# Score differences from subtracted keys, later transposes, a spread split, and top-k values multiplied once a batch

## The reference, cut to what matters

```
x = x + attn_a(ln(x))     # 16 heads of 8: softmax(q k^T) v over 1024 tokens, then Wo
x = x + ffn(ln(x))        # 128 -> 512 -> 512 -> 128, signs as weights, relu between
x = x + attn_b(ln(x))     # 8 heads of 16, windows of 64 tokens, top 32 of each by distance
x = x + ffn(ln(x))
# attn_b, per batch, head and token t
q, v   = relu(x @ encoder_query), relu(x @ encoder_value)
metric = softplus(base + 0.1 * mlp(mean of q))
dist   = sqrt(sum((q[window] - q[t])**2 * metric) + 1e-8)
top 32 nearest: w = exp(-dist) / sum;  context = sum(w * v[of those tokens])
context += gate * 0.1 * (q / |q|) @ (U V);  out = q * context;  out @ decoder
```

## Time and profile before

| | us |
|---|---|
| median of 3 executions (3197.55 to 3203.15) | 3201.6 |
| profiled execution, its own time | 3204.65 |
| its span, first to last instruction | 3202.8 |
| first batch's maximum phase, up to the exponentials | 102.7 |
| a middle batch: maximum phase | 189.0 |
| a middle batch: exponential phase | 174.9 |
| tail behind the last exponential | 294.7 |

### The profile page before, as it was taken

One profiled execution on the slowest core, in us unless ns is written; L12 is line 12 of the kernel. 1 busy time (PEld: TensorE's weight loads), 2 busy tenths in 40 slices (PEclk: granted clock), 3 DMA queues, 4 the chain that ended last, 5 costly groups with the idle time before them and its releaser, 6 DMA issues.

```text
span 3202.8 us, 73054 instructions
## 1 busy us (share of the span) xinstructions
PE 2629.4 (82%) x22579; PEld 1200.3 (37%) x22579; DVE 2128.0 (66%) x10282; ACT 2331.6 (73%) x3225; POOL 618.0 (19%) x797
## 2 busy tenths in 40 slices
PE   5878778889788888888879888898978888887666
PEld 2212243344333443334433344333433344333444
DVE  5701668846776668856689466885677666892595
ACT  4697569967698667976689666996669866795433
POOL 2010013101131112401132011311123111221232
PEclk6599689999899998999989998999989998999888
DMA  2011001000010000100000000000001000000000
GB/s 80 14 36 31 2 1 38 28 15 6 9 35 29 11 6 9 48 22 8 2 33 29 17 9 9 32 28 16 5 9 39 29 10 2 9 2 1 1 8 8
DMA packets 60585, 58.20 MB, mean 18 GB/s; under 512 B 15218, under 2 KB 41524, under 8 KB 60196
## 3 DMA queue, kind: packets, MB, share of 16 engines
q1 hardware_dynamic: 59952, 52.95, 5.3%
q10 hardware_dynamic: 244, 0.39, 0.0%
HBM read 35.66 MB, written 17.56 MB: 17 GB/s over the span
## 4 chain that ended last, share of the span: by engine, by line
PE 40%; ACT 24%; issue 20%; DVE 10%; POOL 4%; SPq 2%; ACTq 0%; DMA 0%; DVEq 0%; POOLq 0%
PE banks L756 37%; ACT PT L1097 11%; ACT pq L1084 3%; POOL Aop L735 2%; DVE pq L1217 2%; PE banks L763 1%; ACT h L1109 1%; ACT xn L1046 1%; DVE xn L1434 1%; DVE h L1437 1%; ACT hparts L1108 1%; ACT h L1156 1%; POOL qkf L709 1%; PE banks L988 1%; SPq L520 1%
## 5 line engine op out<-in xcount | busy, mean ns | idle before, releaser
L1097 ACT ACTIVATE PT<-banks 128x1024 f32<-128x1024 f32 x1024 | 996.4, 1035 | 47.9 <-PE banks L756 38.9
L1217 DVE CUSTOM_DVE_ANT_0 pq<-pq,banks 128x512 f32<-128x512 f32 x1024 | 660.2, 685 | 269.6 <-ACT pq L1084 241.7
L1084 ACT ACTIVATE pq<-banks 128x1024 f32<-128x1024 f32 x512 | 523.5, 1022 | 337.3 <-PE banks L756 328.4
L756 PE MATMUL banks<-K,Q 48*128 48x512 bf16 x3072 | 494.8, 435 | 87.3 <-ACT pq L1084 65.2
L756 PE MATMUL banks<-PT,Vg 128*32 128x512 f32 x4096 | 560.2, 620 | 2.0 <-ACT PT L1097 2.0
L756 PE MATMUL banks<-Q,K 51*128 51x512 bf16 x2048 | 397.6, 396 | 168.0 <-ACT PT L1097 158.8
L719 POOL TENSOR_TENSOR hparts<-h,hparts 128x512 fp32r<-128x512 f32 x112 | 140.3, 1272 | 1152.1 <-ACT h L1109 1152.0
L1434 DVE MATCH_REPLACE8 xn<-h,xn 128x96 f32<-128x96 f32 x1536 | 352.6, 243 | 0.0
L756 PEld LDWEIGHTS banks<-Q,K 51*128 51x128 bf16 x2048 | 108.8, 93 | 590.4 <-issue 560.3
L756 PE MATMUL banks<-hparts,W 128*128 128x512 f32 x1024 | 301.9, 423 | 27.6 <-ACT h L1109 21.7
L756 PEld LDWEIGHTS banks<-K,Q 48*128 48x128 bf16 x3072 | 127.6, 100 | 399.4 <-issue 341.4
(11 more groups left out here) (200 smaller groups left out, 3412.7 us busy)
## 6 DMA issues: line engine op xcount, KB each, us to landing
scratch_qk<-pq SPq DMA_DIRECT2D x24, 512.0 KB, 2.7
qkf<-in_hidden_states SPq DMA_DIRECT2D x16, 512.0 KB, 3.9
Q<-scratch_qk SPq DMA_DIRECT2D x126, 48.0 KB
K<-scratch_qk SPq DMA_DIRECT2D x126, 48.0 KB
Q<-scratch_qk SPq DMA_DIRECT2D x126, 32.0 KB
K<-scratch_qk SPq DMA_DIRECT2D x126, 32.0 KB
out<-xr SPq DMA_DIRECT2D x14, 256.0 KB, 2.3
K<-scratch_qk SPq DMA_DIRECT2D x126, 16.0 KB
```

Of the source, the lines that this page charges most:

```text
L756: return pe.matmul(o, l, r, start=start, stop=stop)
L1084: act.activation(cut(g), ring_pair if work is TURN0 and g % 2 else pair[0], ACT.Relu).then_inc(diff_out.sem, 1)
L1097: act.activation(PT[:, at:at + 2, :], pair[g % ESLOTS], ACT.Exp, scale=1.0 if i % 8 < 4 else -1.0).then_inc(probs.sem, 1)
L1217: dve.tensor_tensor_reduce(r, r, pair[1 + g % 2][:, par, :], 1.0, -3.0e38, ALU.subtract, ALU.max, mred[:, par, i, qt:qt + 1]).then_inc(max ...
```

## The change

**Differences of the keys.** GpSimd adds the halves of the keys (the far half is negated) into `kd`, which is split into three parts as well. K's rows grow from 1024 to 1536 columns, the last 512 being the difference. A group's difference is one pair of products instead of two: four products a group.

**Later transposes.** `mturn` n stands behind group 16(n+1)+1 or so, at 2.1 groups past the quad's end instead of 0.6; the last one stands at 0.02 of the exponential phase.

**Spread split.** The rounding and subtracting of the parts becomes five stages `split` behind `qk`, spaced among the other stages of the exponential phase. The part of the difference adds three half-wide steps on GpSimd and two on ScalarE.

**Values once a batch.** Stage `ev` multiplies all 1024 tokens at once (two banks), evicts them into `vrow` (in `Bs`), and SP writes them to DRAM with a repeated last row; `keys` on VectorE waits for that before it writes `Bs`. Stage `vload` brings the four windows of a unit back, at that unit's first slot. `vw` is gone. `Vg` has 9 columns a head instead of 32, and `pvs` uses 9.

```diff
-            (1, [("pad", 0), ("an", 0)]), (2, [("qtok", 0), ("qtok", 1)]), (4, [("keys", 0)]),
+            (1, [("pad", 0), ("an", 0), ("ev", 0)]), (2, [("qtok", 0), ("qtok", 1)]), (4, [("keys", 0)]),
...
-        (3.0, [(_u >= 2, "decd", _u - 2), (_next, "aop", _u + 1), (_last, "vw", _u - 1), (_here, "top", (_u, 0))]),
+        (3.0, [(_u >= 2, "decd", _u - 2), (_next, "aop", _u + 1), (_here, "vload", _u), (_here, "top", (_u, 0))]),
...
-MROWS = [(x, [("a", stage, n)]) for n in range(NQUAD) for x, stage in
-         ((((n + 1) * QGROUPS - 0.2) / GROUPS, "mrow"), (((n + 1) * QGROUPS + 0.6) / GROUPS, "mturn"))]
+MROWS = [(((n + 1) * QGROUPS - 0.2) / GROUPS, [("a", "mrow", n)]) for n in range(NQUAD)]
+
+MTURNS = [(((n + 1) * QGROUPS + 2.1) / GROUPS, [("a", "mturn", n)]) for n in range(NQUAD - 1)], [(0.02, [("a", "mturn", NQUAD - 1)])]
...
@@ SP
+                    if stage == "ev":
+                        for i in range(2):
+                            sp.wait_ge(*R.moved(c, k + i))
+                        sp.wait_ge(*v_ones.at(b, 1))
+                        for i in range(2):
+                            sp.wait_ge(*v_in[i].at(b, 0))
+                        sp.dma_start(scratch_v[0:T].rearrange("(j p) x -> p j x", p=P),
+                                     vrow.rearrange("p j h e -> p j (h e)")).then_inc(v_out.sem, 16)
+                        sp.dma_start(scratch_v[T:RPAD].unsqueeze(0), ...).then_inc(v_out.sem, 16)
+                    if stage == "vload":
+                        if n == 0:
+                            sp.wait_ge(*v_out.at(b, 2))
+                        if n >= 2:
+                            sp.wait_ge(*R.filled(c, use["pv", n - 2]))
+                        for i in range(NBLK):
+                            sp.dma_start(Vw[:, n % 2, i, :, :].rearrange("p h e -> p (h e)"),
+                                         scratch_v[window(NBLK * n + i)]).then_inc(v_in[n % 2].sem, 16)
@@ GpSimd, stage qk and split
+                        pool.tensor_tensor(kd, qkf[:, 1, 0:HALF], qkf[:, 1, HALF:T], ALU.add).then_inc(kd_a.sem, 1)
...
+                    if (stage, n) == ("split", 0):
+                        pool.wait_ge(*act_a.at(b, 3))
+                        pool.tensor_tensor(kd, kd, parts_of(2, 0), ALU.subtract).then_inc(pool_a.sem, 1)
+                    if stage == "split" and 1 <= n <= 3:
+                        w = n - 1
+                        pool.wait_ge(*act_a.at(b, w + 4))
+                        pool.tensor_tensor(parts_of(w, 2), whole(w), parts_of(w, 1), ALU.subtract).then_inc(pool_a.sem, 1)
@@ TensorE, stage max
-                            if g > 1 and g % QGROUPS == 1:
+                            if g > QGROUPS and g % QGROUPS == 3:
                                 pe.wait_ge(*R.moved(c, use["mturn", n - 1]))
...
-                        near, far = slice(0, HALF), slice(HALF, T)
-                        for dst, keys, start, stop in ((diff, near, True, False), (diff, far, False, True),
-                                                       (pair[1 + g % 2], far, True, True)):
+                        for dst, keys in ((diff, slice(T, KT)), (pair[1 + g % 2], slice(HALF, T))):
...
-                    if stage == "vw":
-                        one(c, k, [(R.bank(k)[0:WW, P * i:P * i + P], xrev[:, window(NBLK * n + i)], ev[:, :], True, True)
-                                      for i in range(NBLK)])
+                    if stage == "ev":
+                        for i in range(2):
+                            one(c, k + i, [(R.bank(k + i)[:, P * q:P * q + P], xrev[:, P * (4 * i + q):P * (4 * i + q) + P], ev[:, :], True, True)
+                                           for q in range(4)])
...
-                        pe.wait_ge(*R.made(c, k, use["vw", n], use["wt", n], use["wt", n] + 1))
+                        pe.wait_ge(*R.made(c, k, use["wt", n], use["wt", n] + 1))
+                        pe.wait_ge(*v_in[n % 2].at(b, n // 2 + 1))
@@ VectorE, stage keys
                         dve.wait_ge(*R.moved(c, use["pad", 0]))
+                        dve.wait_ge(*v_out.at(b, 2))
```

More of the change, by code:

```diff
@@ L35 @@
 MROW = len(QPART) * HD
+KT = T + HALF
 VW = 32
@@ L61 @@
 USES = dict(qk=4, v=2, turn=1, back=1, wo=1, mturn=1, lnT=1, lnTa=2, fa=1, fb=1, fc=1, flip=1, he=1, qd=1, hid=1, mod=1,
-            key=1, pad=1, an=1, qtok=1, hebb=1, dist=2, vw=1, wt=2, pv=1, st=1, dec=1)
+            key=1, pad=1, an=1, qtok=1, hebb=1, dist=2, ev=2, wt=2, pv=1, st=1, dec=1)
 def uses(stage, n):
@@ L173, in phases @@
 def phases(ahead, behind, twice):
-    one, two = [FIRST_V, MAXES, MROWS], [exp_slots()]
+    one, two = [FIRST_V, MAXES, MROWS, MTURNS[0]], [exp_slots(), MTURNS[1]]
     if behind:
@@ L185, in phases @@
     order = merged(*one) + merged(*two)
+    assert not ahead or order.index(("h", "split", 4)) < order.index(("h", "load", 0))
     if twice:
@@ L203, in numbered @@
     return said, use, k
-HEAD = [("h", s, 0) for s in ("ln", "weights", "lnr", "lnf", "lnn", "lnTa", "qk")] + [("h", "load", 0), ("h", "tables", 0)]
-HEAD += [("h", "load", n) for n in range(1, NQUAD)]
+HEAD = [("h", s, 0) for s in ("ln", "weights", "lnr", "lnf", "lnn", "lnTa", "qk")] + [("h", "split", i) for i in range(5)]
+HEAD += [("h", "load", 0), ("h", "tables", 0)] + [("h", "load", n) for n in range(1, NQUAD)]
 TAIL_SPANS = dict(o=(0.000, 0.090), p=(0.075, 0.380), t=(0.380, 1.000), q=(0.380, 0.700), z=(0.723, 0.915))
@@ L401, in hybrid_block_kernel @@
         ones3 = xT[0:PARTS, 0:T // 2].bitcast(BF16)
+        kd = xT[:, HALF:T]
         wload = oT[:, 0, :].rearrange("p (a c) -> p a c", a=8)[:, 0:4, :]
@@ L447, in hybrid_block_kernel @@
         gn_l = count("gate_ln", 1)
+        v_ones = count("value_ones", 1)
+        v_out = count("values_out", 2, 16)
+        v_in = [count(f"values_in{i}", NU // 2, 16 * NBLK) for i in range(2)]
         e_steps = count("e_steps", 2 * NU)
@@ L456, in hybrid_block_kernel @@
         xb_a = count("bias_added", 1)
-        act_a = count("part_rounded", 4)
-        pool_a = count("part_left", 4)
-        split_out = [count(f"split_out{part}", 1, 16) for part in range(PARTS)]
+        act_a = count("part_rounded", 6)
+        pool_a = count("part_left", 6)
+        kd_a = count("keys_subtracted", 1)
+        split_out = [count(f"split_out{part}", 2, 16) for part in range(PARTS)]
         quad_in = [count(f"quad{n}_in", 1, 24 * 16) for n in range(NQUAD)]
@@ L847, in go @@
                                 rows_ = slice(64 * par, 64 * par + MROW)
-                                ins = mm(dst[:, par, :], Q[rows_, n, i, P * qt:P * qt + P], K[rows_, n, i, keys], start, stop)
-                            if stop:
-                                ins.then_inc((diff_in if dst is diff else far_in).sem, 1)
+                                ins = mm(dst[:, par, :], Q[rows_, n, i, P * qt:P * qt + P], K[rows_, n, i, keys])
+                            ins.then_inc((diff_in if dst is diff else far_in).sem, 1)
                     if stage == "mturn":
@@ L1051, in go @@
                     if stage == "lnT":
+                        if work is not LAST and n == ((0, 0) if work is TURN1 else (2, 0)):
+                            act.wait_ge(*pool_a.at(c, 6))
                         evict(c, k, xT_[:, HALF * n[1]:HALF * n[1] + HALF], R.bank(k)[:, :])
@@ L1072, in go @@
                                     act.wait_ge(*split_out[part].at(b, 0))
-                            act.activation(pq[:, 3 * w, :], qkf[:, w, :], ACT.Identity).then_inc(act_a.sem, 1)
-                        for w in range(2):
-                            act.wait_ge(*pool_a.at(b, w + 1))
-                            act.activation(pq[:, 3 * w + 1, :], qkf[:, w, :], ACT.Identity).then_inc(act_a.sem, 1)
+                            act.activation(parts_of(w, 0), qkf[:, w, :], ACT.Identity).then_inc(act_a.sem, 1)
+                    if (stage, n) == ("split", 0):
+                        act.wait_ge(*kd_a.at(b, 1))
+                        act.activation(parts_of(2, 0), kd, ACT.Identity).then_inc(act_a.sem, 1)
+                    if stage == "split" and 1 <= n <= 3:
+                        w = n - 1
+                        act.wait_ge(*pool_a.at(b, w + 1))
+                        act.activation(parts_of(w, 1), whole(w), ACT.Identity).then_inc(act_a.sem, 1)
                     if stage == "max":
@@ L1156, in go @@
                             act.activation(e, e, ACT.Exp, scale=-1.0).then_inc(e_act.sem, 1)
-                    if stage == "vw":
-                        evict(c, k, Vw[:, n % 2, :, :, 0:SE],
-                              R.bank(k)[0:WW, :].rearrange("p (w h e) -> p w h e", w=NBLK, h=SH), ACT.Relu)
+                    if stage == "ev":
+                        for i in range(2):
+                            evict(c, k + i, vrow[:, 4 * i:4 * i + 4, :, 0:SE],
+                                  R.bank(k + i)[:, :].rearrange("p (j h e) -> p j h e", j=4, h=SH), ACT.Relu)
                     if stage == "wt":
```

82 lines of the change are left out of this document (51 added, 31 removed).

## The result

The changed kernel takes 3154.2 us (median of 4 runs, 3144.67 to 3157.13), the kernel before 3202.4 (4 runs, 3197.55 to 3203.15): a ratio of 0.9848, 95% interval 0.9824 to 0.9871, or 48 us less. 109 us less was forecast.

What follows compares the result with a forecast made beforehand. ScalarE was taken to bound the exponential phase, a chain of engines the maximum phase; terms of -66 -5 -15 -36 -38 -2 +42 +6 +5 summed to -109 us, giving 3093 us, own range 3050 to 3140, wider range 3035 to 3162.

Steps and rivals of the forecast that it cites:

- the products' term: Maximum phases: four score products a group instead of six save 9.4 us each, -66 us in seven; second batch -5 more.
- the value wait: Late in the maximum phase VectorE waits for the value rows to leave `Bs`: +6 us a batch, +42; tail +5.
- later transposes: Maximum phase and hand-over: transposes moved later end TensorE's waits for maxima, -5.1 us in each of seven batches, -36.
- values once and spread split: Exponential phases: fewer evictions and no ScalarE wait for GpSimd, -5.5 us each, -38 in seven; first phase -2.
- head: Before the first products: longer split on GpSimd and K loads grown by half, +6 us, ends +3 and +9.
- tail, without the value wait: After the last exponential: the only cost named was VectorE's wait for the value rows, +5 us.
- the cuts of the second batch: Sign of being right: second batch's maximum phase, cuts 1.87 us apart, where they came every 2.30 us.
- exponential phases of 169 us: Sign of being right: exponential phases fall to 169 us, from 174.9 us in a middle batch.
- a maximum phase above 185 us: Sign of being wrong: maximum phases stay above 185 us, against 189.0 us in a middle batch before.
- Rival (a): Maximum phase: ScalarE and VectorE take over, a quarter of the products' gain, value wait 10 us: 3154 us; 0.20 with (d).
- (d): Maximum phase: later transposes only move the waits, to a ring bank, and the 36 us stay: 3129 us; 0.20 with (a).
- Rival (c): Feed-forward groups: TensorE pauses longer and falls to 1.2 GHz; 28% low cancels 109 us, 40% gives 3247 us; chance 0.05.

Runs made afterwards that it cites:

- own_twoprod: `own` with the products of near and far keys summed again instead of single products with the differences: 3133.4 us, ratio 0.9788.
- twoprod: The changed kernel with the products of near and far keys summed again instead of single products with the differences: 3191.6 us, ratio 0.9972.
- own_early: `own` with all four transposes of the maxima back at their old places: 3130.1 us, ratio 0.9785.
- own_last: `own` with only a batch's last transpose of the maxima back at the end of the maximum phase: 3106.7 us, ratio 0.9715.
- novalues: The changed kernel with the values multiplied and evicted unit by unit again in the exponential phase: 3113.2 us, ratio 0.9725.
- own_onego: `own` with the five split steps in one go right behind the evictions of queries and keys, not spread: 3106.8 us, ratio 0.9707.
- own: The changed kernel with value rows in an idle piece of the probabilities' buffer instead of `Bs`, so VectorE no longer waits for their transfer: 3091.5 us, ratio 0.9646.
- own_tlater: `own` with the units' work of the exponential phase beginning some 2.8 us later: 3092.3 us, ratio 0.9661.
- own_aop_tlater: `own` with the units' work 2.8 us later and GpSimd's `Aop` products, but the first two units', five slots sooner: 3075.8 us, ratio 0.9611.

## Why the prediction was wrong, and where it was right

The prediction's sum missed by 61 us, and two of its terms carry the miss: the products' term by 44 us, the value wait by 16. By the medians, against 3091.5 us:

| term | forecast us | measured us | by |
|---|---|---|---|
| single products, first two batches included | -86 less the first batch's transposes | -42 (-37 in the changed kernel) | `own_twoprod`, `twoprod` |
| later transposes | -36 | -39 (last one -15, forecast -19) | `own_early`, `own_last` |
| values once and spread split | -40 | -22 and -15 | `novalues`, `own_onego` |
| head | +6 | +9 (first cut at 54.6; 51.9 to 54.6 in the traces) | trace |
| tail, without the value wait | 0 | +2 (296.4 us after the last exponential, 294.7 before) | trace |
| value wait, middle batches and tail | +42 +5 | +63 (by the traces 57 and 5) | `own` |

Without the last row the measured terms sum to -107 us; the kernel with its own place is 111 us faster than the kernel before. No run takes away the making of the differences (their rounding, subtracting and loading). The forecast's -40 had 8 us of it, so the values and the spread split were forecast at -48 and brought -37.

**The products' term was too large.** The step took half of the removed 18.9 us as the gain of a maximum phase, 9.4 us. At 0.21 us a group that needs 44 of 64 groups to become shorter. (The 0.75 us that the step gives for three pairs would be 0.64 by the same 0.21; nothing rests on it.) At the same clock 27 intervals of a phase do, for 6.3 us, and waits that did not shrink take 1.1 us of it. The other intervals, in which the clocks differ, come out 0.3 us a phase longer. Together the six last phases gain 4.9 us each, about the quarter (4.7 us) that the step had named as the least. Had the 70 intervals with differing clocks gained as the 308 others did, it would be 6.3 us a phase; so the clock costs about 1.5 us a phase, which is an estimate from these intervals. Outside the maximum phases 5.7 us are given back, most of it at the hand-overs and in the exponential phases. In the second batch 14.3 us came, forecast 14.4, and its cuts stand 1.87 us apart, as forecast. In the first, 10 us came where 15 were forecast, 5.8 by the products and some 4.5 by the transposes (94.0 us with them back, 89.5 without); VectorE is busy 83.49 of 92.35 us there, so it is nearly the bound, as said.

**The value wait was mis-sized.** The step said +6 us a batch, with an end of +10. The mechanism was as described, down to group 61's far products. From the end of the second eviction (1186.94) to VectorE's start the sum had 0.7 us for SP and 2.7 for the landing; it is 5.1 us in every one of the eight batches, 1.7 more. The landing was taken from one other transfer, and for the large transfer: that takes 3.5 us, and the small one behind it, which the step counted at nothing, 4.2. The Trainium skill's "DMA: Bandwidth & Descriptors", section "Anatomy of one DMA — SWDGE (gpsimd) path", by whose fit I had estimated 3.3 us for the large one, was nearer than the row that I preferred; for the small one the fit gives an estimate of about 2.1, and the trace does not agree. So VectorE waits 8.0 us on the mean of seven batches, not 6.5, and a maximum phase is 8.2 us longer, 7.7 of it in group 62's interval. The tail's 4.8 us are the +5 of the forecast.

**The transposes.** The prediction says that the last cut ends at 1235.48. That is the end of VectorE's last reduction; the cut ends at 1233.00. The sum holds with the right name: the exponentials' products wait for that reduction, in the changed kernel too, and the first exponential starts about 0.65 us behind it. The hand-over is 3.6 us where 3.1 was forecast.

**The exponential phases.** ScalarE's work fell by 4.4 us (the step had 4.8 less 1.2), but the phase by 1.4. The step named GpSimd's wait that goes and not the ones that come: TensorE at `Aop`, behind the earlier hand-over and behind the split's subtractions. `own_tlater` and `own_aop_tlater` show it: with the later start alone nothing is gained, with `Aop` sooner as well the same work takes 168.5 us.

Of the prediction's own signs, the number of score products, the cuts of the second batch and TensorE's wait for `mb` (none but 0.4 us in the first batch) came as said. The exponential phases of 169 us did not come (173.5), and a sign of being wrong did, a maximum phase above 185 us (187.4).

Rival (a), at 0.20 together with (d), gave 3154 us, which is the measured time. Its quarter of the products' gain is what the six last phases show. Its value wait of 10 us a batch is too dear (8.2), and the first batch, the hand-overs and the exponential phases, which it left as they were, make up for that; that it meets the time to the microsecond is luck. Rival (c), the clock, came only in small part: 0.92 in the maximum phase against 0.93, and 0.94 in the exponential phase against 0.96. But between groups 6 and 49 of the six last phases the two kernels with summed products beside the rest of the change (`twoprod`, `own_twoprod`) keep the full clock throughout, while the changed kernel and `own` have 3.4 to 10.2 us at the lower one in every phase (the kernel before: none to 6.8 us). Why was not tested. Rival (d) fell with the transposes' 39 us.

## What to carry to other kernels

A buffer borrowed for a transfer out is busy until the transfer has landed: before it is borrowed, look who writes it next, and put the transfer several steps ahead of that or take a place that is idle for the rest of the stage. Count the groups in which the saved instruction is on the chain before you multiply: here 27 intervals of a phase became shorter, not 44. Before intervals of two kernels are compared, set apart those in which their clocks differ. Price a wait for two transfers by the one that lands last, the small one too. When a shorter stage lets the next one begin sooner, look at the third engine that feeds it.

## What the runs showed of the hardware

A VectorE step of 128 x 4 elements took 1.14 us, not 0.17, when it began 0.15 us after a GpSimd `tensor_tensor`; it ended at 1018.14, GpSimd's first of two (2.49 us together) at about 1018.10. Begun 0.26, 0.35 and 0.47 us after it, the same step took 1.03, 0.94 and 0.83 us: it ended 1.3 us after GpSimd's start each time. In the kernel with its own place this falls once at the start and once later in each of the middle batches (1.14 to 1.16 and 0.83 or 0.84 us), in the kernel before once a batch (1.04 or 1.05). The Trainium skill's "SBUF — State Buffer", section "SBUF: two separate sides", states that a GpSimd instruction and a VectorE one in a two-port mode share a port pair as an exclusive lock, which the one that starts first holds for its whole instruction. The times agree; no row shows the step's mode. The order of two starts 0.2 us apart decides on 1 us of VectorE.

The size of a transfer says little of its landing here: 34 KB read from one partition took 4.2 us, right behind 544 KB that took 3.5; 384 KB (`scratch_k`) took 3.2, and 512 KB before the change 2.7. How the 34 KB would do alone was not tried.
